# A graph network's edge ordering in batches of eight columns, a shorter mish, and scatters spread over three stages

## The reference

```python
# layer 1, for every edge: eight relations, four bases, a weight; then summed by destination
m = sum_b comp[type, b] * (h @ basis[b])[src];  m = m * edge_weight
# layer 3, for every edge, with mish(x) = x * tanh(softplus(x))
first = mish(concat(h[src], h[dst], edge_attr_64) @ W1 + b1)
total = segment_sum(mish(first @ W2 + b2), dst)
```

## Time and profile before

| | us |
|---|---|
| median of 3 runs (lowest, highest) | 2321.59 (2320.09, 2327.09) |
| the profiled execution | 2321.93 |
| its span, first to last instruction | 2320.2 |
| mean granted TensorE clock, 1 is full speed | 0.965 |

### The profile page before, as it was taken

The page is one execution under the profiler, slowest core; times in us unless marked ns, Lnnn a source line. Parts: engine busy times, 40 slices in busy tenths (PEclk is TensorE's granted clock), DMA queues, the critical chain, the costliest instruction groups (busy, mean ns, idle before and its releaser), DMA issues. The chain is left out here.

```text
span 2320.2 us, 36936 instructions
## 1 busy us (share of the span) xinstructions
PE 2040.2 (88%) x11455; PEld 1110.0 (48%) x11455; DVE 1774.4 (76%) x3095; ACT 1455.3 (63%) x2429; POOL 1291.1 (56%) x1065
## 2 busy tenths in 40 slices
PE   0787688789988949999999987999999999999965
PEld 0433677546655624444444453455555554555422
DVE  8999899853333358888888853999999999999723
ACT  1999777521112225555555533999999999999822
POOL 0576677518720035444444204788888888888530
PEclk9999899889989979999999999999999999999988
DMA  2410100102143335433333304232222222222000
GB/s 115 165 28 14 55 0 0 59 31 78 41 117 95 90 92 158 131 100 101 93 93 96 71 15 135 87 92 77 77 72 77 77 72 77 77 68 81 10 0 22
DMA packets 81562, 170.33 MB, mean 73 GB/s; under 512 B 17378, under 2 KB 43221, under 8 KB 80449
## 3 DMA queue, kind: packets, MB, share of 16 engines
q0 software_dynamic: 35840, 98.88, 15.6%
q1 hardware_dynamic: 45624, 70.25, 9.0%
HBM read 144.93 MB, written 23.98 MB: 73 GB/s over the span
## 5 line engine op out<-in xcount | busy, mean ns | idle before, releaser
L884 PE MATMUL e_two_ps<-w,e_first 128*128 128x512 bf16 x1408 | 419.9, 380 | 0.1
L1631 ACT ACTIVATE u_msg<-u_t,slot_record 128x128 f32<-128x128 f32 x704 | 223.3, 390 | 93.3 <-DVE u_t L1687 93.3
L643 POOL DMA_INDIRECT sorted_records<-edge_record,slot_row x160 | 210.2, 1314 | 126.9 <-issue 57.7
L884 PE MATMUL e_two_ps<-w,e_first_low 128*128 128x512 bf16 x704 | 267.3, 380 | 0.0
L1816 POOL TENSOR_TENSOR e_first_low<-e_first 128x1024 bf16<-128x1024 f32 x88 | 250.1, 2842 | 21.9 <-DVE e_first L2007 21.9
L1821 POOL TENSOR_TENSOR e_msg_low<-e_act 128x1024 bf16<-128x1024 f32 x88 | 225.5, 2562 | 56.2 <-DVE e_act L2019 55.3
L1549 POOL DMA_INDIRECT u_got<-up_table,u_idx x176 | 186.0, 1057 | 76.8 <-issue 42.9
L2312 POOL DMA_INDIRECT e_got<-src_table,e_idx x176 | 186.7, 1061 | 70.5 <-issue 35.4
L884 PEld LDWEIGHTS e_two_ps<-w,e_first 128*128 128x128 bf16 x1408 | 134.5, 98 | 148.6 <-issue 2.2
L685 PE MATMUL pairs_ps<-cell_high,src_hot 128*128 128x144 bf16 x1180 | 153.8, 227 | 44.3 <-POOL cell_rest L709 22.3
L1595 PE MATMUL u_sum_ps<-u_msg,u_hot 128*125 128x512 f32 x352 | 185.2, 608 | 3.4 <-ACT u_msg L1631 3.4
(11 more groups left out here) (366 smaller groups left out, 5144.4 us busy)
## 6 DMA issues: line engine op xcount, KB each, us to landing
conv_w<-in_L_gnn_basis_dram SPq DMA_DIRECT2D x8, 1024.0 KB, 5.5
sorted_records<-pairs SPq DMA_DIRECT2D x5, 1408.0 KB, 10.9
edge_record<-in_edge_floats_dram SPq DMA_DIRECT2D x2, 3125.0 KB
later_w<-in_L_gnn_W_dram SPq DMA_DIRECT2D x6, 1024.0 KB
attr_parts<-h SPq DMA_DIRECT2D x22, 256.0 KB, 2.1
e_attrT<-attr_parts SPq DMA_DIRECT2D x44, 128.0 KB
e_dst_all<-dst_row SPq DMA_DIRECT2D x44, 125.0 KB
pairs<-in_edge_floats_dram SPq DMA_DIRECT2D x1, 3125.0 KB
```

Source lines behind the costliest of these rows:

```text
L643: pg.nc.gpsimd.indirect_dma_start(out=pg.sorted, out_offset=bass.IndirectOffsetOnAxis(ap=pg.slot_row[:, j:j + 1], axis=0), in_=pg.edge_rec ...
L884: last = nc.tensor.matmul(out, lhsT, rhs, start=(n == 0), stop=(n == len(pairs) - 1))
L1631: last = nc.scalar.activation(msg[:, k, at * MUL:(at + 1) * MUL], t12[:, k % 2, of], ACT.Copy, scale=pg.record[:, bass.ds(t, 1), Y + m])
```

## The change

In the ordering, eight columns are worked on at a time: 20 batches with two sets of buffers, laid out as four pairs of columns side by side, so that the two columns of a pair are neighbours in memory and the innermost dimension of each operand is that pair. VectorE makes lane and tile one-hots as comparisons of two tensors (a doubled count `iota_twice` and the numbers of the columns, repeated by a step of 0 in a middle dimension), and both key parts and two of the three weight parts as products with the lane's one-hot. ScalarE keeps the third weight part and clears a piece of `pairs` after each batch from the fifth on. TensorE reads both operands with a step of two elements. GpSimd clears 12800 words of each row of `pairs` ahead of its scatters, scatters 64 columns, waits for `placed` and clears the last 4960 words. Another 16 columns are scattered in layer 0 (5 before its bias additions, 11 behind them), and 80 in the first convolution, the last 16 of these after a second load by SyncE and a copy by ScalarE (`name_ends`).

In mish the clamp becomes e(e+2) on VectorE, the squaring on ScalarE is gone, and the logarithm takes a scale and a bias that keep it in range. TensorE reads the rows of the destination block out of `by_dst` directly, with an offset that its own sequencer loads for each unit; the copy on VectorE is gone. The four one-hots of `hot_rows` become one operation of two tensors, and `hot_columns` compares two tensors. Two memsets and two iotas are added on GpSimd; some arrays change to 2-byte types. Core of the diff:

```diff
+FIRST = 64
+BATCH = 8
-GROWN = float(np.exp(LIMIT))
+LOG_SCALE = 0.75 * 2.0 ** -64
+LOG_BIAS = 2.0 * LOG_SCALE
+SHARE_BIAS = float(np.log(2.0) + np.log(LOG_SCALE))
...
+    pg.last_ends = pg.sb("last_ends", [EP, EARLY - FIRST, 2], ctx=pg.pair_keep)
-    pg.pair_lane = pg.sb("pair_lane", [EP, EC], ctx=pg.pair_once)
-    pg.pair_tile = pg.sb("pair_tile", [EP, EC], ctx=pg.pair_once)
-    pg.key_part = pg.sb("key_part", [EP, 2, EC], ctx=pg.pair_once)
+    pg.pair_lane = pg.sb("pair_lane", [EP, EC], BF16, pg.pair_once)
+    pg.pair_tile = pg.sb("pair_tile", [EP, EC], BF16, pg.pair_once)
+    pg.key_part = pg.sb("key_part", [EP, 2, EC], FP16, pg.pair_once)
...
             nc.gpsimd.memset(zero[:, :], 0.0).then_inc(zeroed, 1)
+            nc.gpsimd.memset(pairs[:, 0:CLEARED], 0.0)
             pool.wait_ge(pg.emptied, 16 * 5)
-            scatter_records(pg, range(0, EARLY))
-            pool.wait_ge(decoded, 1)
-            pairs = pg.pairs[:, :, :, :].rearrange("p s n d -> p (s n d)")
-            size = pairs.shape[1] // 4
-            for n in range(1, 4):
-                nc.gpsimd.memset(pairs[:, n * size:(n + 1) * size], 0.0)
+            scatter_records(pg, range(0, FIRST))
+            pool.wait_ge(placed, 1)
+            nc.gpsimd.memset(pairs[:, HOTS:], 0.0)
 
...
-            for i in range(EC // STRIDE):
-                for n in range(STRIDE):
-                    s = n % 4
-                    pe.wait_ge(keys_hot, STRIDE * i + n + 1)
+            for i in range(BATCHES):
+                s = i % 2
+                pe.wait_ge(keys_hot, i + 1)
+                for j in range(BATCH):
                     for c in range(2):
-                        nc.tensor.matmul(column(c), key_hot[:, s, c, :], tile_hot[:, s, :], start=False, stop=False)
-                    pe.wait_ge(weights_hot, STRIDE * i + n + 1)
-                    for c in range(3):
-                        last = nc.tensor.matmul(column(2 + c), weight_hot[:, s, c, :], tile_hot[:, s, :],
-                                                start=False, stop=False)
-                    last.then_inc(free, 1)
+                        nc.tensor.matmul(column(c), key_hot[:, s, c, j // 2, :, j % 2],
+                                         tile_hot[:, s, j // 2, :, j % 2], start=False, stop=False)
+                pe.wait_ge(weights_hot, i + 1)
+                for j in range(BATCH):
+                    for c in range(2):
+                        nc.tensor.matmul(column(2 + c), weight_hot[:, s, c, j // 2, :, j % 2],
+                                         tile_hot[:, s, j // 2, :, j % 2], start=False, stop=False)
+                pe.wait_ge(rests_hot, i + 1)
+                for j in range(BATCH):
+                    last = nc.tensor.matmul(column(4), rest_hot[:, s, j, :], tile_hot[:, s, j // 2, :, j % 2],
+                                            start=False, stop=False)
+                last.then_inc(free, 1)
...
-            for i in range(EC // STRIDE):
-                for n in range(STRIDE):
-                    s = n % 4
-                    j = STRIDE * i + n
-                    act.wait_ge(lanes_hot, j + 1)
-                    act.wait_ge(free, j + 1)
-                    for c in range(3):
-                        last = nc.scalar.activation(weight_hot[:, s, c, :], lane_hot[:, s, :], ACT.Copy,
-                                                    scale=pg.weight_part[:, c, bass.ds(j, 1)])
-                    last.then_inc(weights_hot, 1)
-            act.wait_ge(pg.emptied, 16 * 5)
-            pairs = pg.pairs[:, :, :, :].rearrange("p s n d -> p (s n d)")
-            size = pairs.shape[1] // 4
-            nc.scalar.activation(pairs[:, 0:size], pg.ones[:, 0:1].broadcast_to([P, size]), ACT.Copy, scale=0.0)
+            size = (HOTS - CLEARED) // (BATCHES - WAITED)
+            for i in range(BATCHES):
+                act.wait_ge(lanes_hot, i + 1)
+                act.wait_ge(free, i + 1)
+                for j in range(BATCH):
+                    last = nc.scalar.activation(rest_hot[:, i % 2, j, :], lane_hot[:, i % 2, j // 2, :, j % 2], ACT.Copy,
+                                                scale=pg.weight_part[:, 2, bass.ds(BATCH * i + j, 1)])
+                last.then_inc(rests_hot, 1)
+                if i >= WAITED:
+                    act.wait_ge(pg.emptied, 16 * 5)
+                    at = CLEARED + (i - WAITED) * size
+                    to = pairs[:, at:at + size]
+                    nc.scalar.activation(to, pg.ones[:, 0:1].broadcast_to(list(to.shape)), ACT.Copy, scale=0.0)
...
-            for i in range(EC // STRIDE):
-                for n in range(STRIDE):
-                    s = n % 4
-                    j = STRIDE * i + n
-                    dve.wait_ge(free, j + 1)
-                    nc.vector.tensor_scalar(lane_hot[:, s, :], pg.iota_lane[0:EP, 0:P],
-                                            pg.pair_lane[:, bass.ds(j, 1)], None, ALU.is_equal).then_inc(lanes_hot, 1)
-                    nc.vector.tensor_scalar(tile_hot[:, s, :], pg.iota_lane[0:EP, :],
-                                            pg.pair_tile[:, bass.ds(j, 1)], None, ALU.is_equal)
-                    for c in range(2):
-                        last = nc.vector.tensor_scalar(key_hot[:, s, c, :], pg.iota_lane[0:EP, 0:P],
-                                                       pg.pair_lane[:, bass.ds(j, 1)], pg.key_part[:, c, bass.ds(j, 1)],
-                                                       ALU.is_equal, ALU.mult)
-                    last.then_inc(keys_hot, 1)
+            def over(x, size):
+
+                return x.rearrange("p (q a j) -> p q a j", a=1, j=2).broadcast_to([EP, TWOS, size, 2])
+
+            def numbers(size):
+
+                return pg.iota_twice[0:EP, 0:size, :].rearrange("p (a l) j -> p a l j", a=1)\
+                    .broadcast_to([EP, TWOS, size, 2])
+
+            for i in range(BATCHES):
+                s = i % 2
+                at = slice(BATCH * i, BATCH * (i + 1))
+                dve.wait_ge(free, i + 1)
+                nc.vector.tensor_tensor(lane_hot[:, s, :, :, :], numbers(P), over(pg.pair_lane[:, at], P),
+                                        ALU.is_equal).then_inc(lanes_hot, 1)
+                nc.vector.tensor_tensor(tile_hot[:, s, :, :, :], numbers(PT), over(pg.pair_tile[:, at], PT),
+                                        ALU.is_equal)
+                dve.wait_ge(lanes_hot, i + 1)
+                for c in range(2):
+                    last = nc.vector.tensor_tensor(key_hot[:, s, c, :, :, :], lane_hot[:, s, :, :, :],
+                                                   over(pg.key_part[:, c, at], P), ALU.mult)
+                last.then_inc(keys_hot, 1)
+                for c in range(2):
+                    last = nc.vector.tensor_tensor(weight_hot[:, s, c, :, :, :], lane_hot[:, s, :, :, :],
+                                                   over(pg.weight_16[:, c, at], P), ALU.mult)
+                last.then_inc(weights_hot, 1)
...
+def late_records(pg, sp, begin, end):
+
+    sp.dma_start(pg.edge_record[0:EP, begin:end, :],
+                 pg.inp["edge_floats"].rearrange("(p j) r -> p j r", j=EC)[:, EARLY + begin:EARLY + end, :])\
+        .then_inc(pg.record_in, 16)
+
...
+def name_ends(pg, begin, ends):
+
+    for n, column in enumerate((SRC, DST)):
+        last = pg.nc.scalar.copy(pg.edge_record[0:EP, begin:begin + ends.shape[1], column], ends[:, :, n])
+    return last
...
-            sp.wait_ge(pg.scattered, 16 * EARLY)
-            sp.dma_start(pg.edge_record[0:EP, 0:EC - EARLY, :],
-                         pg.inp["edge_floats"].rearrange("(p j) r -> p j r", j=EC)[:, EARLY:EC, :])\
-                .then_inc(pg.record_in, 16)
+            sp.wait_ge(pg.scattered, 16 * FIRST)
+            late_records(pg, sp, 0, FIRST)
...
+            scatter_records(pg, range(FIRST, FIRST + 5))
             pool.wait_ge(bias_in, 16)
             for b in range(NB):
                 nc.gpsimd.tensor_tensor(pg.x[:, b, :], pg.x[:, b, :], bias[:, :], ALU.add).then_inc(biased, 1)
+            scatter_records(pg, range(FIRST + 5, EARLY))
...
+                sp.wait_ge(pg.scattered, 16 * EARLY)
+                late_records(pg, sp, FIRST, EARLY)
...
-                scatter_records(pg, range(EARLY, EC))
+                scatter_records(pg, range(EARLY, EARLY + FIRST))
+                pool.wait_ge(ends_named, 1)
+                scatter_records(pg, range(EARLY + FIRST, EC))
...
+                if c == 0 and n == NB:
+                    act.wait_ge(pg.record_in, 32)
+                    name_ends(pg, FIRST, pg.last_ends).then_inc(ends_named, 1)
...
+                at = nc.tensor.value_load(pg.block_of_group[0:1, bass.ds(g, 1)], min_val=0, max_val=NB - 1)
                 pe.wait_ge(mish1_ready, n + 1)
                 if u == 0:
                     pe.wait_ge(hotT_ready, g + 3)
-                    pe.wait_ge(dst_ready, g + 1)
                     pe.wait_ge(attr_in[h], (g - h) * 16 + 32)
```

(55 more changed lines are left out.)

127 lines of the change are left out of this document (71 added, 56 removed).

## The result

The changed kernel takes 2287.64 us (median of 4 runs, 2285.57 to 2289.18), 0.9847 of the kernel before (95% interval 0.9833 to 0.9861) beside which it was timed (2321.81, four runs by then): 34 us less. The profiled execution has a span of 2287.4 us against 2320.2. The forecast was 2279 in a range of 2258 to 2308: the sign and the range held, the gain was put 8.6 us too large, and most of it came where it was forecast.

What follows compares the result with a forecast made beforehand. ScalarE was taken to set the ordering's pace, with VectorE close behind, and TensorE to bound the edge pass. From 2321.9 us, 38 for the ordering and 4.6 for the edge pass were subtracted, giving 2279; range 2258 to 2308.

Steps and rivals of the forecast that it cites:

- Pace of VectorE and TensorE: Ordering: a batch of eight columns takes VectorE 4.11 us and TensorE 4.2, with decoding starting at about 153 instead of 209.3.
- GpSimd's row: Ordering: scatters wait for VectorE's running two-source operation, mean 2.0 us; scatters end at 200, the last clearing at 204.
- The stage's end: Ordering: GpSimd ends it, and the next stage starts at 205.4 instead of 243.5, a gain of 38 us.
- Layer 0: Layer 0: 16 scatters moved in cost 0, with 5 ahead making the bias additions about 4 us late; 4 us allowed.
- Edge pass: Edge pass: 1.1 us less for the copy, 2.3 at the start and 1.2 at the end; sum -4.6, between -1 and -7.
- Steady part: 0, TensorE bound: Edge pass between start and end: no time gained, since TensorE bounds it; size 0.
- C: Ordering: VectorE's unbroken operations shut GpSimd's scatters out, time 2317 or 2345 us; chance 0.09.
- E: Ordering: each scatter also holds VectorE for 1.06 us, 68 us in all, time 2329; chance 0.04.
- F: Edge pass: the block number's loads show on TensorE, up to 48 us, time 2283 to 2327; chance 0.06.
- D: Ordering: VectorE's paired operations run at one element a step, 155 us in all, time 2332; chance 0.06.
- G: Ordering: a few of GpSimd's scatters are held for longer, time 2290 to 2305 us; chance 0.06.
- B: Ordering: GpSimd isn't held by VectorE's operations, so decoding ends last at 187, time 2262 us; chance 0.15.

Runs made afterwards that it cites:

- the second profile: The changed kernel with nothing changed, profiled once more on the first of the three chips of the experiments: 2288.42 us.

## Why the prediction was right, and where it was not

**Pace of VectorE and TensorE.** A batch was put at 4.11 us of VectorE and 4.2 of TensorE. The first two batches, which wait for nothing, start 4.07 apart (65.39 and 69.46), the steady ones 4.21. The third starts 1.6 late, since VectorE waits for TensorE there, so that decoding began at 155.7 and not 153. The step that took the earlier trace rows and not the earlier trace rows for paired operands was right, and the run without pairs shows that the earlier trace rows would have held otherwise. Operations of 1024 elements start 0.60 us apart with pairs and 1.14 without (0.69 and 1.21 long). The Trainium skill, "VectorE: DVE Perf Modes", section on what auto-detection checks, gives tensor_tensor the double rate where every tensor is 16-bit with a step of one; both runs agree with it.

**GpSimd's row.** 35 scatters before 148 were forecast, 35 had begun by then; 2.0 us each, and it was 2.10 in the steady batches; the last was to end at 200 and ended at 199.2; the clearing at 204, and it was 203.4. This was the longest chain of the argument, and its numbers held. Its premise, that a waiting scatter is let in when the running operation ends, is not general: without pairs it would have given a scatter for nearly every operation, and one took 143 us. Nothing in the argument told the two cases apart, so that part was luck. The Trainium skill, "SBUF — State Buffer", section on the two separate sides, has a port pair that is locked for the whole instruction and a loser that waits. The split of layer 0, held until the additions were over, agrees with a lock, but it waited over several instructions and the scatter of 143 us over some hundred; the rule doesn't say why a scatter gets in between some back-to-back operations and not between others.

**The stage's end, a wait that was mis-sized.** 1.4 us from the last operation to the next stage was read from a stage that VectorE ends. With GpSimd last it was 3.5. With the clearing 0.6 earlier than forecast that is 1.5 of the missing gain (206.9 for 205.4).

**Layer 0, the step that failed.** "5 of them stand ahead of its bias additions, about 4 us late then, for additions wanted some 16 us later": the 4 us were right and the cover was right for the additions' reader. VectorE's two-source split was not looked at, which starts at 456.07 in the kernel before, just as the additions end. Cost 0 was 3.5 in this profile, and 1.9 in the second, where the split took 7.15; the allowance of 4 us stood in the range.

**Edge pass.** -4.6 was forecast and -7.8 measured. Start: 24.0 to 19.4, which is 4.6 for the 3.4 of the sum (1.1 for the copy, 2.3 for two squarings). The missing microsecond lies ahead of the first exponential: products of 0.38 us, those of the higher level, begin 3.2 us behind the first product (1391.36) and 5.1 behind it before (1424.67). In the second profile, and in that of the kernel without pairs, the start is 20.4 and the pass 801.8 and 801.7, so this microsecond is chance. End: -1.2 as forecast, and "the units before wait for the bias addition and POOL's low part instead, so nothing more" held: those waits are three of 2.37 us and one of 4.96 in both kernels. "Steady part: 0, TensorE bound" was the wrong step: the waits for the low part there fell by 2.4 us. Start, steady part and end make 8.2; a wait ahead of the third group's first product grew from 1.2 (for its one-hots) to 1.9. The profile names nobody for the 1.9, but the one-hots of that group take 2.12 us beside GpSimd's low part and end at 1413.00, 0.2 ahead of the product. So no wait of TensorE for its block loads is seen, as forecast.

**Tail and convolutions.** 5.3 and 2.1 us that no step of the prediction had. One of its own signs of being wrong was "if another stage moves by over 4 us", and the tail did. The tail goes with the edge pass, by the granted clock; the convolutions took 345.5 to 351.1 us over the profiles with the same instructions there, so 2 us are within what one execution shows. Since the tail's loss and the 3.2 us that the pass gained beyond its forecast partly cancel, the total looks better than its terms.

**Rivals.** C (scatters shut out) was closer than its chance said: it is what the same batches do without pairs. E (a scatter holds VectorE for its whole time) is out in the ordering: the batches are 4.06 us long with two scatters in each, where TensorE was made faster, and 4.07 ahead of the first scatter. But layer 0 shows that GpSimd's additions with two sources do hold a two-source operation of VectorE. F and D didn't come. G (a few scatters held for longer) didn't either: the longest took 4.0 us, and the row ended in time. B is out: a scatter took 2.10 with its issue.

## What to carry to other kernels

When a one-hot or any product with a repeated number is batched, two neighbours in the innermost dimension, each its own number, gave 0.60 us where a step of 0 gave 1.14. When work is moved on GpSimd, ask not only who reads it but which two-source operation of VectorE it will now run beside: 6 us of additions moved by 4 cost 3.5. In this kernel a stage that GpSimd ends cost 1.4 to 3 us more behind its last row than one that VectorE ends. And where TensorE bounds a stage, a wait can cost more than its length: behind two waits of 2.4 and 2.5 us came 1.7 us of slower products each, though not behind every wait of that length.

## What the runs showed that was not expected

- One scatter of GpSimd lasted 143.11 us beside VectorE operations of 1.2 and 2.1 us without a pause.
- The kernel before has an ordering of 178.5 us in its first measurement and 202.7 on the first chip of the experiments, by TensorE's granted clock (1.00, and 0.83 to 0.87) in a loop that leaves it idle for 6 of 40 us.
- A tail of 160 products takes 96.2 to 98.1 us or 100.1 to 101.9 with the same instructions, by what the pass ahead of it was.
- Squaring put back into the pass costs it 13.8 us, though the earlier trace rows show TensorE full with it. With squaring and direct rows the pass is 6 longer than with squaring and the copy (before). Its waits for the low part between the start and the last groups are 7.5 us then, 5.2 before and 2.8 after, and the rest of the 6 is TensorE's lower level behind such waits.
